# AdaLN-style adapter layer and LoRA feed-forward layer on one core: where the column registers are loaded, where the second chunk's weights are rounded, and where the bin sort runs

## The chip, the cores and the metric

One core of a Trainium2 chip runs the whole kernel. The metric is the device time of one execution in microseconds (us). The engines are named as in the profile: PE (matrix products) and PEld (its weight loads), DVE, ACT, POOL and SP. Each engine has its own instruction queue (DVEq, ACTq and so on), which also runs the register instructions. All engines work in parallel and meet only at semaphores.

## The reference

The input x has 64 items of 32 tokens with 512 features. Each item picks one of 8 weight matrices for the first layer (`a0`, values 3 to 7) and one of 16 adapters for the second (`a1`, values 2 to 6). Cut to what matters:

```python
# first layer
h0 = einsum('bsi,boi->bso', x, L0_cond_weight[a0])               # one 512x512 matrix per item
x  = x + h0 @ kernel + bias + lora(h0; 8 groups of 8 items) + shared_lora(h0)
# second layer: gated feed-forward, 512 -> 1376 -> 512, each product with the item's rank-16 adapter
gate = x @ W_gate.T + 0.5 * B_gate[a1] @ (A_gate[a1] @ x)
up   = x @ W_up.T   + 0.5 * B_up[a1]   @ (A_up[a1] @ x)
act  = silu(gate) * up
h    = act @ W_down.T + 0.5 * B_down[a1] @ (A_down[a1] @ act)
# routed linear layer: softmax over 4 ranks, top 1 selects a LoRA of that rank
out  = x + h @ W.T + b + routed_lora(h)
```

Which items share an adapter is data, so the kernel sorts the items on the chip and reaches an item's tokens through a column number that it holds in a register.

## The kernel before, in words

**Numbers.** Every fp32 operand is split in two fp32r parts, hi (rounded, written by ACT with `high`) and lo (the rest, x minus hi, written by DVE or POOL with `low`). A product is three matmuls (`product`, L1303 to L1305: hi*hi, lo*hi, hi*lo); a product with a small left side that holds hi and lo one above the other is two (`stacked`, L1309 and L1310).

**Stage 1, conditioning.** DVE sorts the 64 items by weight matrix into 22 blocks of 4 items (some slots are empty). For each block b, ACT and DVE load four column numbers (`item_cols`, L417) and split the block's tokens (`high_xs`, `low_xs`), PE multiplies (`cond`, L1373 to L1375: 12 matmuls), ACT (even b) or DVE (odd b) copies the result out, and POOL scatters it to a DRAM scratch. Between these, DVE runs a second sort, the bin sort, which puts the items in the order of the second layer's adapters: `fill_bins` ahead of block 0 (L1004), `find_fillers`, `rank_items`, `place_fillers`, `place_items` at blocks 13 to 16, then two small matmuls on PE after block 20 (L1384 to L1387), `item_places` and `gather_rows`. Each step of a sort waits for the one before it (`then`). The second block's tokens are split after block 0's weights, and `scatter_rows` lies between block 0's tokens and its weights.

**Stage 2, first layer.** Four passes t of 512 tokens (`first_layer`): PE transposes h0, multiplies it with the dense kernel and adds the LoRA part; DVE adds bias and residual (`add(0)` to `add(3)`). PE transposes the adapter rows of the second layer (`turn_a`) only after the four passes.

**Stage 3, second layer.** Four token blocks t of 512 tokens, each with 11 chunks fc of 128 hidden features (`chunks` calls `step`; chunk n = 11t + fc). A block opens with its tokens gathered in sorted order and split (`high_x1` on ACT, `low_x1` on DVE, 16 column slices each), `high_at`/`low_at`, then `ranks` and the masks (`open_tg`). Each chunk: PE transposes adapter rows (`turn_down`, L1515), gate product, up product, adapter parts, and the down product of the chunk before; ACT rounds the chunk's weights (`high_gu`, `high_bu`), `ad`, `dn`, computes silu and rounds act; DVE computes `low_bu`, lo of ad, act_f and act_lo; POOL computes gu_lo and dn_lo and issues the gathers of adapter rows two chunks ahead (`rows`). After the last chunk PE finishes block t (`td`, `bd`), ACT and DVE spread h back to the tokens' places (`put_h`, 16 column copies each), and only then do they begin the chunks of block t+1. In `high_x1`, `low_x1` and `put_h` the 16 column numbers are loaded four at a time (`bin_cols`, L423) between the slices. PE may not write the down product of block t+1 before `put_h(t)` is through (L1545, L1546).

**Stage 4, routed linear layer** (`routed`, `second_layer`), four passes of 512 tokens, which starts when `put_h(3)` is done.

The order on each engine is the order in which the code is written; nothing is planned at run time. The queues wait at semaphores in that order.

Of the kernel before, what the change touches and what calls it, by code (L numbers as in the profile page):

```python
# [21 lines left out]
F32 = mybir.dt.float32  # L22
# [103 lines left out]
def two_layers(nc, a, out):  # L126
    with ExitStack() as ctx:
# [127 lines left out]
        below = sb("below", [P, 2, N_ADP], F32)  # L255
        least = sb("least", [P, NBIN], F32)
        short = sb("short", [P, NBIN], F32)
        short_h = sb("short_h", [P, NBIN], F32)
        room = sb("room", [P, NBIN], F32)
        step_z = sb("step_z", [P, NBIN], F32)  # L260
# [4 lines left out]
        first4 = sb("first4", [P, NBIN], F32)  # L265
        end4 = sb("end4", [P, NBIN], F32)
# [363 lines left out]
        def _(act):  # L630
# [18 lines left out]
            def high_xs(b):  # L649
                at = item_cols(act, b)  # L650
# [20 lines left out]
            high_xs(1)  # L671
# [38 lines left out]
            high_h0(0)  # L710
# [12 lines left out]

# [15 lines left out]
            def high_x1(t):  # L739
# [12 lines left out]
            def put_h(t):  # L752
                act.wait_ge(S["h_ps"], C * t + 2)
                for q in range(TB // BT):
                    at = bin_cols(act, t * (TB // BT) + q)
                    for j in range(BI):
                        i = (q * BI + j) * ITEM_T
                        act.activation(h_all[:, 0:2, bass.ds(at[j], ITEM_T)], psD[:, 0:2, i:i + ITEM_T], ACT.Copy
                                       ).then_inc(S["h_out0"], 1)
# [9 lines left out]
            def body(t):  # L769
                def step(fc, j, par):  # L770
# [9 lines left out]
                    high(dn_hi[:, par, :], dn_raw[:], S["dn_hi_s"])  # L780
# [899 lines left out]
```

## Time and profile before

| | us |
|---|---|
| median of 3 runs (lowest, highest) | 784.01 (783.42, 784.02) |
| the profiled execution's own time | 782.84 |
| its span, first to last instruction | 780.9 |
| PE busy in the span | 704.9 (90%) |
| PEld, DVE, ACT, POOL busy | 586.1, 368.3, 289.4, 322.4 |

A row of a timeline or group has the start or the busy time in us, the engine, the line of the kernel, the operation, what it writes and reads, how many instructions (x4), and in brackets how long the engine had been idle before it and what ended that. "issue" means that the profile shows no other engine that it waited for. A line can be that of a helper (L838 is DVE's `low`, L632 ACT's `high`, L547 POOL's `low`), so tiles tell more. PEclk is PE's granted clock as a share of full speed; its two levels are 1.2 and 2.4 GHz (0.5 and 1.0).

### The profile page before, as it was taken

What the parts mean: (1) busy time and instruction counts of PE and PEld (TensorE: products, weight loads), DVE (VectorE), ACT (ScalarE), POOL (GpSimd) and SP (SyncE); (2) the same over time, 40 slices, a digit from 0 to 9 for tenths busy, and PEclk for the clock granted to TensorE, in tenths of its full rate; (3) what the DMA queues carried; (4) which work ended last, traced back from release to release, by engine and by line L of the source; (5) the groups of instructions that cost most, each with busy time, mean ns of one, the idle gap of its engine ahead of it and who ended that gap; (6) DMA issues with size and microseconds to landing.
All of it is one profiled execution on the core that took longest, in us unless ns stands there. A gap on an engine that the chain in (4) does not pass through costs nothing.

```text
span 780.9 us, 11491 instructions
## 1 busy us (share of the span) xinstructions
PE 704.9 (90%) x3432; PEld 586.1 (75%) x3432; DVE 368.3 (47%) x714; ACT 289.4 (37%) x605; POOL 322.4 (41%) x266
## 2 busy tenths in 40 slices
PE   4799899996999996799999779999977999977997
PEld 3577788875788885688888667888766888865775
DVE  5787755436424424533442554344254344324655
ACT  2775442115433324434332353333334433213220
POOL 0134350002876652385666167666318666400000
PEclk9999999997999998899999889999988999997999
DMA  8865271001443352143334124433314333200112
GB/s 321 320 226 187 98 282 55 1 0 42 136 151 122 121 195 72 49 134 122 121 121 131 45 71 140 130 117 99 125 41 122 121 122 121 74 0 2 55 55 107
DMA packets 30800, 88.90 MB, mean 114 GB/s; under 512 B 4608, under 2 KB 4736, under 8 KB 29216
## 3 DMA queue, kind: packets, MB, share of 16 engines
q1 hardware_dynamic: 21936, 61.05, 22.9%
q0 software_dynamic: 8672, 27.27, 10.8%
q8 instruction: 22, 0.36, 0.2%
q14 instruction: 26, 0.21, 0.1%
q10 hardware_dynamic: 144, 0.00, 0.0%
HBM read 78.35 MB, written 9.96 MB: 113 GB/s over the span
## 4 chain that ended last, share of the span: by engine, by line
PE 75%; DVE 9%; issue 5%; DVEq 4%; ACT 2%; ACTq 2%; DMA 1%; POOL 0%; SPq 0%; POOLq 0%
PE psD L1303 8%; PE psD L1304 8%; PE psD L1305 8%; PE psG L1303 5%; PE psG L1304 5%; PE psG L1305 5%; PE psU L1303 5%; PE psU L1304 5%; PE psU L1305 5%; DVEq L423 2%; PE psX L1303 2%; PE psX L1304 2%; PE psX L1305 2%; DVE tm L1142 2%; PE psD L1373 2%
## 5 line engine op out<-in xcount | busy, mean ns | idle before, releaser
L547 POOL TENSOR_TENSOR gu_lo<-gu_raw,gu_hi 128x1024 fp32r<-128x1024 f32 x44 | 105.7, 2402 | 211.2 <-ACT gu_hi L632 210.9
L838 DVE TENSOR_TENSOR bu<-ab,bu 64x512 fp32r<-64x512 f32 x44 | 84.2, 1913 | 66.3 <-ACT bu L632 66.0
L582 POOL DMA_INDIRECT ab<-in_ab,idx_row x88 | 87.0, 989 | 47.8 <-POOL idx_row L576 34.3
L1199 DVE TENSOR_TENSOR act_f<-psU,silu 128x512 f32<-128x512 f32 x44 | 30.3, 689 | 142.7 <-ACT silu L783 142.7
L783 ACT ACTIVATE silu<-psG 128x512 f32<-128x512 f32 x44 | 26.4, 599 | 158.8 <-PE psG L1310 158.7
L547 POOL TENSOR_TENSOR dn_lo<-dn_raw,dn_hi 128x512 fp32r<-128x512 f32 x44 | 69.2, 1572 | 26.2 <-ACT dn_hi L632 26.2
L1303 PE MATMUL psG<-x_hi,gu_hi 128*128 128x512 f32 x176 | 76.1, 432 | 0.0
L1304 PE MATMUL psG<-x_lo,gu_hi 128*128 128x512 f32 x176 | 71.9, 408 | 0.0
L1305 PE MATMUL psG<-x_hi,gu_lo 128*128 128x512 f32 x176 | 71.7, 407 | 0.0
L1303 PE MATMUL psD<-act_hi,dn_hi 128*128 128x512 f32 x176 | 69.0, 392 | 0.0
L1303 PE MATMUL psU<-x_hi,gu_hi 128*128 128x512 f32 x176 | 69.0, 392 | 0.0
L1304 PE MATMUL psD<-act_lo,dn_hi 128*128 128x512 f32 x176 | 69.0, 392 | 0.0
L1305 PE MATMUL psD<-act_hi,dn_lo 128*128 128x512 f32 x176 | 68.7, 390 | 0.0
L1304 PE MATMUL psU<-x_lo,gu_hi 128*128 128x512 f32 x176 | 68.6, 389 | 0.0
L1305 PE MATMUL psU<-x_hi,gu_lo 128*128 128x512 f32 x176 | 68.5, 389 | 0.0
L552 POOL DMA_INDIRECT h_scratch<-h,idx_s x22 | 25.5, 1161 | 68.7 <-DVE h L1033 34.9
L632 ACT ACTIVATE gu_hi<-gu_raw 128x1024 fp32r<-128x1024 f32 x44 | 46.2, 1050 | 3.3 <-DMA gu_raw<-in_gu 3.3
L632 ACT ACTIVATE act_hi<-act_f 128x512 fp32r<-128x512 f32 x44 | 27.8, 632 | 47.7 <-DVE act_f L1199 47.7
L1373 PE MATMUL psD<-cond_w_hi,xs_t_hi 128*128 x88 | 36.6, 416 | 9.5 <-DVE cond_w_lo L838 7.4
L838 DVE TENSOR_TENSOR act_lo<-act_f,act_hi 128x512 fp32r<-128x512 f32 x44 | 30.6, 695 | 30.7 <-ACT act_hi L632 30.7
L1305 PEld LDWEIGHTS psG<-x_hi,gu_lo 128*128 128x128 f32 x176 | 35.0, 199 | 8.4
L1304 PEld LDWEIGHTS psG<-x_lo,gu_hi 128*128 128x128 f32 x176 | 35.2, 200 | 6.1
(321 smaller groups left out, 1622.9 us busy)
## 6 DMA issues: line engine op xcount, KB each, us to landing
gu_raw<-in_gu SPq DMA_DIRECT2D x44, 512.0 KB, 3.5
dn_raw<-in_dn SPq DMA_DIRECT2D x44, 256.0 KB, 3.1
cond_w_raw<-in_cond_w SPq DMA_DIRECT2D x8, 1024.0 KB, 5.7
x_all<-in_x_t SPq DMA_DIRECT2D x4, 1024.0 KB, 9.9
tok<-h_scratch SPq DMA_DIRECT2D x4, 1024.0 KB, 7.2
out_t<-x_all SPq DMA_DIRECT2D x16, 256.0 KB, 2.2
ab<-in_ab,idx_row POOLq DMA_INDIRECT x88, 3.2
kraw<-in_kern SPq DMA_DIRECT2D x1, 1024.0 KB, 12.3
```

Of the source, the lines that this page charges most:

```text
L423: _, at = nc.values_load_multi_w_load_instructions(item1_at[0:1, b * BI:b * BI + BI], engines=[eng.engine], min_val=0, max_val=TOKENS - IT ...
L547: pool.tensor_tensor(dst, x, hi, ALU.subtract).then_inc(s, 1)
L552: pool.indirect_dma_start(h0_dram, bass.IndirectOffsetOnAxis(idx_s[:, b:b + 1], 0), h0[:, ring, :], None).then_inc(S[f"c_st{ring}"], 16)
L582: pool.indirect_dma_start(ab[:, par, g, :], None, a["ab"], bass.IndirectOffsetOnAxis(idx_row[:, par, g:g + 1], 0)).then_inc(S[f"ab_in{par} ...
L632: act.activation(dst, x, ACT.Copy).then_inc(s, 1)
L783: act.activation(silu[:], psG[:], ACT.Silu).then_inc(S["silu_s"], 1)
L838: dve.tensor_tensor(dst, x, hi, ALU.subtract).then_inc(s, 1)
L1199: dve.tensor_tensor(act_f[:], psU[:], silu[:], ALU.mult).then_inc(S["act_f_s"], 1)
L1303: pe.matmul(ps, wh, xh, start=start, stop=False, skip_group_check=True)
L1304: pe.matmul(ps, wh, xl, start=False, stop=False, skip_group_check=True)
L1305: return pe.matmul(ps, wl, xh, start=False, stop=stop, skip_group_check=True)
L1373: pe.matmul(ps, xh, w[0], start=c == 0, stop=False)
```

## The change

The bin sort leaves stage 1 except for its two counts, which are copied to tiles of their own (`keep_counts`). `count_bins` runs after stage 1, the other parts in the gaps of the four passes of stage 2, and the two small matmuls go to PE between `kern(0)` and `kern(1)` of the last pass. In front of block 0 both engines load the columns of two blocks first, then split both blocks' tokens, then the weights; `scatter_rows` goes ahead of the tokens. The last pass of stage 2 takes in `turn_a(0)` on PE, and `block_cols`, `low_at(0)` and `low_bu(0, 0)` on DVE. `block_cols` loads all 16 columns of a token block at once: for `high_x1`/`low_x1(t+1)` in chunk 9 of block t, for `put_h(t)` in chunk 10, ahead of the wait for silu's input. ACT rounds gu of chunk 0 of block t+1 after td_hi, and gu and bu of its chunk 1 before `put_h(t)` and no longer in chunk 0. The kernel adder of stage 1 moves from block 11 to 12.

```diff
+        rank1 = sb("rank1", [ITEMS, N_ADP], F32)
+        count1 = sb("count1", [P, N_ADP], F32)
...
-        def bin_cols(eng, b):
-
-            _, at = nc.values_load_multi_w_load_instructions(item1_at[0:1, b * BI:b * BI + BI], engines=[eng.engine],
-                                                             min_val=0, max_val=TOKENS - ITEM_T)
-            return at
+        def block_cols(eng, t):
+
+            cols = []
+            for b in range(TB // BT * t, TB // BT * (t + 1)):
+                _, at = nc.values_load_multi_w_load_instructions(item1_at[0:1, b * BI:b * BI + BI], engines=[eng.engine],
+                                                                 min_val=0, max_val=TOKENS - ITEM_T)
+                cols += at
+            return cols
...
             act.wait_ge(S["item_ready"], 1)
-            act.wait_ge(S["x_all_in"], 16 * NTB)
-            high_xs(0)
+            cols = item_cols(act, 0), item_cols(act, 1)
             folded(2)
             folded(3)
+            act.wait_ge(S["x_all_in"], 16 * NTB)
+            high_xs(0, cols[0])
+            high_xs(1, cols[1])
             act.wait_ge(S["w_in0"], 16)
...
-                for q in range(TB // BT):
-                    at = bin_cols(act, t * (TB // BT) + q)
-                    for j in range(BI):
-                        i = (q * BI + j) * ITEM_T
-                        high(x1_hi[:, :, i:i + ITEM_T], x_all[:, :, bass.ds(at[j], ITEM_T)], S["x1_hi_s"])
+                for j, col in enumerate(at):
+                    i = j * ITEM_T
+                    high(x1_hi[:, :, i:i + ITEM_T], x_all[:, :, bass.ds(col, ITEM_T)], S["x1_hi_s"])
...
             act.wait_ge(S["item1_ready"], 1)
+            taken = block_cols(act, 0)
             high_at(0)
             high_gu(0, 0, 0)
             high_bu(0, 1)
-            high_x1(0)
+            high_x1(0, taken)
             high_tg(0, 0)
             high_tg(0, 1)
+            high_gu(1, 1, 0)
+            high_bu(1, 1)
...
-                    if not last(fc):
+                    if not first and not last(fc):
                         high_gu(1 - par, n + 1, n)
                         high_bu(1 - par, (NF // 2 + par) * t + j + par + 1)
...
+                    if last(fc, 1) and t < NTB - 1:
+                        taken.extend(block_cols(act, t + 1))
+                    if last(fc):
+                        placed.extend(block_cols(act, t))
                     act.wait_ge(S["gate_ps"], n + 1)
...
                 if t < NTB - 1:
-                    high_x1(t + 1)
+                    high_x1(t + 1, taken)
                     high_at(t + 1)
-                    high_gu(0, NF * t + NF, NF * t + NF)
                 act.wait_ge(S["td_m"], t + 1)
                 high(td_hi[:], tm[:, 1, :], S["td_hi_s"])
                 if t < NTB - 1:
+                    high_gu(0, NF * t + NF, NF * t + NF)
                     high_bu(0, (NF // 2 + 1) * (t + 1) + 1)
                     high_tg(t + 1, 0)
                     high_tg(t + 1, 1)
-                put_h(t)
+                    high_gu(1, NF * t + NF + 1, NF * t + NF)
+                    high_bu(1, NF // 2 * (t + 1) + 1)
+                put_h(t, placed)
...
             dve.wait_ge(S["item_ready"], 1)
-            low_xs(0)
+            cols = item_cols(dve, 0), item_cols(dve, 1)
             scatter_rows()
+            keep_counts()
+            low_xs(0, cols[0])
+            low_xs(1, cols[1])
...
-                if b == 11:
+                if b == 12:
...
-                if b == 13:
-                    find_fillers()
-                if b == 14:
-                    rank_items()
-                if b == 15:
-                    dve.wait_ge(S["small_in"], 32)
-                    place_fillers()
-                if b == 16:
-                    place_items()
...
+                if t == 0:
+                    fill_bins()
+                if t == 1:
+                    gather_rows()
+                    rank_items()
+                if t == 2:
+                    place_items()
+                if t == 3:
+                    item_places()
                 add(0)
                 add(1)
                 if t < NTB - 1:
                     low_h0(t + 1)
+                else:
+                    taken.extend(block_cols(dve, 0))
+                    low_at(0)
+                    low_bu(0, 0)
                 add(2)
+                if t == 0:
+                    find_fillers()
+                if t == 1:
+                    dve.wait_ge(S["small_in"], 32)
+                    place_fillers()
                 add(3)
...
-            pe.wait_ge(S["item1_ready"], 1)
-            pe.wait_ge(S["mask1_ready"], 1)
...
                 kern(0)
+                if t == NTB - 1:
+                    pe.wait_ge(S["t0_m"], NTB)
+                    pe.wait_ge(S["perm1_s"], 1)
+                    pe.matmul(psX[:, 0:ITEMS], cst("item_no", ITEMS), perm1[:], start=True, stop=True)
+                    pe.matmul(psX[:, ITEMS:2 * ITEMS], cst("ones", ITEMS), perm1_f[:], start=True, stop=True
+                              ).then_inc(S["pos1_ps"], 1)
                 kern(1)
...
                 if t < NTB - 1:
                     turn_h0(t + 1)
+                else:
+                    turn_a(0)
```

DVE's `body` changes as ACT's does (`block_cols(dve, ...)` stands between the lo part of ad and the wait for silu), and `low_x1` and `put_h` take the list of columns in the same way.

## Rows read from the trace of the kernel before

**Rows 1.** Page, part 2: PE's granted clock in 40 slices of 19.5 us, tenths.

```profile
PEclk9999999997999998899999889999988999997999
```

**Rows 2.** PE's waits, whole span: us in total, times, longest.

```profile
PE psX L1515 <- DVE ad L838: 17.9, 6, 4.9
PE psX L1303 <- DVE at_lo L838: 17.8, 3, 7.5
PE psX L1303 <- DVE hta_lo L838: 10.0, 1, 10.0
...
PE psD L1373 <- DVE cond_w_lo L838: 7.4, 1, 7.4
```

**Rows 3.** Windows: us, then busy of PE, PEld, DVE, ACT, POOL, PEclk, DMA, GB/s.

```profile
286.50:340.10 53.60, 41.20 (x207) 35.56 (x206) 25.35 (x54) 20.41 (x56) 21.72 (x18) 0.87 0.28 89
419.20:471.90 52.70, 41.09 (x208) 35.10 (x206) 28.42 (x56) 22.32 (x58) 23.38 (x18) 0.87 0.23 71
551.00:602.70 51.70, 41.74 (x208) 35.96 (x207) 24.02 (x54) 20.68 (x57) 21.76 (x19) 0.87 0.23 71
```

**Rows 4.** Windows: a stretch inside a block, narrow matmuls, a slow-clock stretch.

```profile
220.00:290.00 70.00, 70.00 (x355) 59.26 (x355) 25.48 (x29) 25.29 (x43) 44.18 (x38) 1.00 0.44 147
...
313.00:316.00 3.00, 3.00 (x27) 3.00 (x26) 2.60 (x4) 0.63 (x1) 0.00 (x0) 1.00 0.00 0
...
327.70:333.00 5.30, 5.29 (x14) 4.24 (x15) 1.15 (x2) 2.63 (x3) 4.21 (x5) 0.50 0.69 213
```

**Rows 5.** DVE timeline, chunks 9 and 10 of block 0: act_f.

```profile
283.59 0.69 DVE L1199 TENSOR_TENSOR act_f<-psU,silu 128x512 f32<-128x512 f32 x1 [4.22 <-ACT silu L783]
...
293.47 0.69 DVE L1199 TENSOR_TENSOR act_f<-psU,silu 128x512 f32<-128x512 f32 x1 [5.87 <-ACT silu L783]
```

**Rows 6.** Line 423, whole span: the queue's load of four columns, ns.

```profile
L423 DVEq TENSOR_LOAD <-item_at x32: 339/343/355, 175.8 to 703.9; - x32
```

**Rows 7.** DVE timeline at the first block change.

```profile
302.98 3.04 DVE L838 TENSOR_TENSOR x_lo<-x_all,x_hi 128x128 fp32r<-128x128 f32 x4 [1.14 <-issue]
...
317.57 0.69 DVE L838 TENSOR_TENSOR bu<-ab,bu 64x512 fp32r<-64x512 f32 x1
...
320.50 0.62 DVE L1170 COPY h_all<-psD 128x64 f32 x4 [1.40 <-issue]
```

**Rows 8.** ACT timeline, same stretch.

```profile
321.11 0.57 ACT L758 ACTIVATE h_all<-psD 128x64 f32 x4 [1.07 <-issue]
```

**Rows 9.** DVE timeline: low_bu of chunk 2 beside POOL; wf_lo in block 2.

```profile
334.85 3.38 DVE L838 TENSOR_TENSOR bu<-ab,bu 64x512 fp32r<-64x512 f32 x1 [5.30 <-ACT bu L632]
...
462.41 7.41 DVE L838 TENSOR_TENSOR wf_lo<-wf_raw,wf_hi 128x2048 fp32r<-128x2048 f32 x1 [2.90 <-ACT rb L632]
```

**Rows 10.** PE timeline, where block 0's ranks begin.

```profile
181.19 0.55 PE L1303 MATMUL psX<-x_hi,at_hi 128*128 128x256 f32 x1 [6.15 <-DVE x_lo L838]
```

**Rows 11.** The first weight load, SP's queue: issue, and time to landing.

```profile
L464 SPq DMA_DIRECT2D cond_w_raw<-in_cond_w x1: 383/383/383, 12.5 to 12.5; - x1
...
DMA to landing us min/median/max: 7.5/7.5/7.5
```

**Rows 12.** Timeline of the opening: ACT's first tokens, DVE's first weights.

```profile
19.06 0.91 ACT L632 ACTIVATE xs_t_hi<-x_all 128x128 fp32r x4 [6.97 <-issue]
...
23.39 2.49 DVE L838 TENSOR_TENSOR cond_w_lo<-cond_w_raw,cond_w_hi 128x512 fp32r<-128x512 f32 x4
```

**Rows 13.** PE timeline: first matmul of conditioning blocks 1, 14 and 21.

```profile
29.49 0.39 PE L1373 MATMUL psD<-cond_w_hi,xs_t_hi 128*128 x1
...
65.82 0.46 PE L1373 MATMUL psD<-cond_w_hi,xs_t_hi 128*128 x1
...
89.21 0.50 PE L1373 MATMUL psD<-cond_w_hi,xs_t_hi 128*128 x1
```

**Rows 14.** DVE timeline, pass 0: the gap before add(0).

```profile
115.78 1.41 DVE L1101 SCALAR_TENSOR_TENSOR x_all<-psD,bias,x_all 128x512 f32<-128x512 f32 x2 [3.09 <-PE psD L1310]
```

**Rows 15.** Window of the second half of fill_bins (eleven small DVE instructions).

```profile
16.20:18.60 2.40, 0.73 (x2) 0.01 (x1) 2.16 (x11) 0.00 (x0) 0.00 (x0) 1.00 1.04 428
```

More of the change, by code:

```diff
@@ L708, in high_h0, with high_gu, high_bu, high_at @@
                     high(HT0[t % 2][0][:, c, :], H0_BANK[c][:], S["h0t_hi"])
+            def high_gu(par, n, free):
+                act.wait_ge(S["gu_in"], 16 * (n + 1))
+                act.wait_ge(S["up_ps"], free)
+                high(gu_hi[:, par, :], gu_raw[:], S["gu_hi_s"])
+            def high_bu(par, gathers):
+                act.wait_ge(S[f"ab_in{par}"], 16 * NGT * gathers)
+                high(bu[:, par], ab[:, par, :, P:STAB], S["bu_hi_s"])
+            def high_at(t):
+                for g in range(NGT):
+                    act.wait_ge(S["at_ps"], NGT * t + g + 1)
+                    high(at_hi[:, g, :], A_BANK[g][:], S["at_hi_s"])
             high_h0(0)
@@ L750, in high_tg, with put_h @@
                 high(tg_hi[:, k, :], tm[:, k, :], S["tg_hi_s"])
-            def put_h(t):
+            def put_h(t, at):
                 act.wait_ge(S["h_ps"], C * t + 2)
[L754 to L759, printed above, removed]
+                for j, col in enumerate(at):
+                    i = j * ITEM_T
+                    act.activation(h_all[:, 0:2, bass.ds(col, ITEM_T)], psD[:, 0:2, i:i + ITEM_T], ACT.Copy
+                                   ).then_inc(S["h_out0"], 1)
             act.wait_ge(S["item1_ready"], 1)
+            taken = block_cols(act, 0)
             high_at(0)
@@ L909, in _, with keep_counts, count_bins @@
             across = [P, NBIN, N_ADP]
-            def fill_bins():
+            def keep_counts():
+                dve.wait_ge(S["count1_ps"], 1)
+                both(dve.tensor_copy(rank1[:], psU[0:ITEMS, 0:N_ADP]),
+                     dve.tensor_copy(count1[:], psU[:, N_ADP:2 * N_ADP]))
+            def count_bins():
                 then(dve.tensor_tensor(tri[:], cst("adapter_no").unsqueeze(1).broadcast_to(across),
                                        cst("adapter_no").unsqueeze(2).broadcast_to(across), ALU.is_le))
-                dve.wait_ge(S["count1_ps"], 1)
-                count = psU[:, N_ADP:2 * N_ADP]
-                then(dve.tensor_scalar(miss[:, 1], count, float(-BI), 0.0, ALU.add, ALU.max))
-                then(dve.scalar_tensor_tensor(out=miss[:, 0], in0=miss[:, 1], scalar=float(BI), in1=count,
+                then(dve.tensor_scalar(miss[:, 1], count1[:], float(-BI), 0.0, ALU.add, ALU.max))
+                then(dve.scalar_tensor_tensor(out=miss[:, 0], in0=miss[:, 1], scalar=float(BI), in1=count1[:],
                                               op0=ALU.add, op1=ALU.subtract))
@@ L951, in rank_items @@
             def rank_items():
-                then(dve.tensor_tensor(qm[:], psU[0:ITEMS, 0:N_ADP], room[0:ITEMS], ALU.add))
+                then(dve.tensor_tensor(qm[:], rank1[:], room[0:ITEMS], ALU.add))
                 then(dve.tensor_tensor(qo[:], qm[:], onehot1[:], ALU.mult))
@@ L1128, in low_at, with low_bu, low_x1 @@
                     low(at_lo[:, g, :], A_BANK[g][:], at_hi[:, g, :], S["at_lo_s"])
-            def low_x1(t):
-                for q in range(TB // BT):
-                    at = bin_cols(dve, t * (TB // BT) + q)
-                    for j in range(BI):
-                        i = (q * BI + j) * ITEM_T
-                        dve.wait_ge(S["x1_hi_s"], TB // ITEM_T * t + q * BI + j + 1)
-                        low(x1_lo[:, :, i:i + ITEM_T], x_all[:, :, bass.ds(at[j], ITEM_T)],
-                            x1_hi[:, :, i:i + ITEM_T], S["x1_lo_s"])
+            def low_bu(par, n):
+                dve.wait_ge(S["bu_hi_s"], n + 1)
+                low(bu[HALF:P, par], ab[HALF:P, par, :, P:STAB], bu[HALF:P, par], S["bu_lo_s"])
+            taken = []
+            for t in range(NTB):
+                first_layer(t)
+            def low_x1(t, at):
+                for j, col in enumerate(at):
+                    i = j * ITEM_T
+                    dve.wait_ge(S["x1_hi_s"], TB // ITEM_T * t + j + 1)
+                    low(x1_lo[:, :, i:i + ITEM_T], x_all[:, :, bass.ds(col, ITEM_T)], x1_hi[:, :, i:i + ITEM_T],
+                        S["x1_lo_s"])
             def masked(dst, ps, r, t, s):
@@ L1162, in open_tg, with put_h @@
                 low_tg(t, 1)
[L1164 removed]
+            def put_h(t, at):
                 dve.wait_ge(S["h_ps"], C * t + C)
[L1166 to L1173 removed]
+                for j, col in enumerate(at):
+                    i = j * ITEM_T
+                    dve.tensor_copy(h_all[:, 2:4, bass.ds(col, ITEM_T)], psD[:, 2:4, i:i + ITEM_T]
+                                    ).then_inc(S["h_out1"], 1)
             dve.wait_ge(S["x1_f"], C * NTB)
[L1175 to L1176 removed]
+            low_x1(0, taken)
             dve.wait_ge(S["mask1_ready"], 1)
             open_tg(0)
[L1180 to L1184 removed]
             def body(t):
+                taken, placed = [], []
                 def step(fc, j, par):
@@ L1195, in step @@
                         S["ad_lo_s"])
+                    if last(fc, 1) and t < NTB - 1:
+                        taken.extend(block_cols(dve, t + 1))
+                    if last(fc):
+                        placed.extend(block_cols(dve, t))
                     dve.wait_ge(S["silu_s"], n + 1)
@@ L1222, in body @@
                     low_bu(0, NF * t + NF)
-                put_h(t)
+                put_h(t, placed)
             for t in range(NTB):
@@ L1456, in first_layer @@
                 lora(3)
-            for t in range(NTB):
-                first_layer(t)
             def turn_a(t):
@@ L1470, in turn_a @@
                     mm.then_inc(S["at_ps"], 1)
+            for t in range(NTB):
+                first_layer(t)
             def ranks(t):
-                pe.wait_ge(S["t0_m"], NTB)
+                pe.wait_ge(S["item1_ready"], 1)
+                pe.wait_ge(S["mask1_ready"], 1)
                 pe.wait_ge(S["ad_lo_s"], NF * t)
@@ L1483, in ranks @@
                 mm.then_inc(S["tg_ps"], 1)
-            turn_a(0)
             ranks(0)
```

60 lines of the change are left out of this document (14 added, 46 removed).

## The prediction

> **What bounds the kernel now.** I read the page first. PE is busy 90% of the span, and the row of its granted clock has dips that come back at even distances [rows 1]. Then PE's waits: the reader is to see four causes, which do not lie in the chunks but between stages: ad_lo (17.9 us in 6 waits), at_lo (17.8 in 3), hta_lo (10.0, once), the first weights (7.4, once) [rows 2]. Inside a block PE never waits: 70 us of 70 at full clock [rows 4], and a chunk takes 293.47 - 283.59 = 9.88 us [rows 5]. So the time to win lies at the three block changes, at the two ends of the second layer, and in conditioning.
>
> The windows from the last chunk's `turn_down` to that of chunk 2 of the next block show what one change costs: 53.6, 52.7 and 51.7 us with the clock at 0.87 on average [rows 3]. Their work on PE at full clock is three chunks (29.6), 48 matmuls of 256 columns for `ranks` and `bd` (27 matmuls take 3.0 us [rows 4], so 5.8 with their weights) and 8 transposes (0.9): 36.3 us. The other 15 to 17 us are a wait for x1_lo and at_lo (5 to 7.5), a wait for ad_lo behind `put_h` (4.6 to 4.9), and PE at 1.2 GHz when it comes back [rows 2, 4]: in 327.7 to 333.0 it is at 0.5 and does 14 matmuls in 5.3 us.
>
> What makes both waits long is not the slices themselves. The four copies of a `put_h` group take 0.62 us, then DVE idles 1.40 and ACT 1.07 with no releaser [rows 7, 8]: that is the queue loading four columns, of which the load proper is 0.343 [rows 6]. A group costs 2.0 us on DVE and 1.6 on ACT, so 16 slices take 8.1 and 6.5.
>
> **The block changes.** (1) `block_cols` costs 4 x about 1.5 = 6.0 us of DVE's queue and 4 x about 1.24 = 5.0 of ACT's (the idle above plus some 0.1 to set up the first slice). It lies in chunks 9 and 10 between ad and silu's wait. There DVE idles 4.2 us in chunk 9, after a low_bu during which the queue is already free (2.5 us), and 5.87 in chunk 10 [rows 5]; DVE's next instruction is due 6.1 us after the queue is free, so the loads fit with 0.1 to 0.2 us to spare. If they overrun, act_f(10) comes late by the overrun, and with it the chain below. Cost taken: 0. (2) The slices then follow each other every 0.2 us: 16 in 3.2 us. Worked from the end of act_lo(10) at 295.5: x1_lo done at 298.8, td mask 299.4, at_lo 300.6. PE ends the last down product at 300.6, so `ranks` starts at about 300.8 and not at 308.1. Since high_gu(0) now stands behind td_hi, POOL's gu_lo no longer falls on the last x_lo slices, which took 3.04 us for four [rows 7]. (3) ranks and bd run at full clock to 306.6; tg_lo is done 4.3 us after ranks (as before), at 308.2; gu_hi(1), bu_hi(1) at 309; `put_h` runs 309 to 311 on both engines; low_bu(1) and ad_lo(0) end at 312.2, and PE asks for ad_lo(0) at 313.1. The second wait is gone, and with it the second slow stretch. (4) Chunk 2: its low_bu waits for the gather (about 319.3) and meets POOL's gu_lo and dn_lo back to back, as in the 3.38 us of [rows 9]; ad_lo(1) at about 323.4 against PE's 323.1: 0.3 us.
>
> So a change takes 36.3 + about 0.7 for starts and the first wait + 0.3 = 37.3 us, against 53.6 and 51.7: -16.3 and -14.4. At the second change DVE also computes wf_lo, 7.4 us because POOL holds it off [rows 9]. With chunk 1 at full clock PE comes for chunk 2 two us sooner, and DVE has wf_lo, ra_lo, rb_lo and low_bu ahead of ad_lo(1). Best case no wait (-15.4), worst 3.6 us (-11.8); I take -13.4. Sum of the three: -44.1.
>
> Here the Trainium skill bears on the trace (SBUF — State Buffer, Who interferes with whom): a DVE instruction with two SBUF inputs and a GpSimd one that reads SBUF exclude each other for the whole instruction, and whoever starts first wins. It speaks against this change, which brings gu_lo(1) forward onto low_bu(0) and low_bu(1). This trace agrees, 0.69 us becoming 3.38.
>
> The same skill (DMA: Bandwidth & Descriptors, Latency and other measured facts) gives a `tensor_load` floor of about 600 ns; the row has 343. By the page `block_cols` would overrun its cover by some 1 us and the sum would be 3 us smaller; the row decides.
>
> **The start.** Before: x_all is there, ACT loads columns, splits block 0 at 19.06, folds, rounds weights from 20.8; DVE has fill_bins (2.2 us of it in [rows 15]), its columns, block 0's lo, then scatter_rows, so w_lo starts at 23.39 and PE at 24.32 [rows 12]. The first weights land at 12.5 + 7.5 = 20.0 [rows 11]. After: columns are loaded by 16.6, scatter_rows and keep_counts done by 18.9, both blocks' lo by 20.6, w_hi of the first quarter 20.05 to 20.7, w_lo from 20.75. PE starts at 21.7: -2.6.
>
> **Conditioning's tail.** Blocks 1 to 14 take (65.82 - 29.49)/13 = 2.79 us each, blocks 14 to 21 (89.21 - 65.82)/7 = 3.34 [rows 13], since the chained sort steps keep DVE's queue from loading columns ahead. Without them PE sets the pace: 7 x 0.55 = 3.8, and 0.6 for the two matmuls taken out; the wait for g_lo returns about 0.2 less: -4.4 in all (the 0.6 is within 3.54 of the last block). kfold's adder at block 12 is covered by two blocks of slack.
>
> **The four passes.** DVE idles 3.09 us before add(0) [rows 14], about 2.4 before add(3). fill_bins takes 2.4, find_fillers 2.1, gather_rows with rank_items 2.1, place_fillers 1.1, place_items 1.2: each fits its gap. Cost 0; without the cover up to 1 us per pass. POOL's gathers for block 0 start some 30 us later but are due 25 us after that. The two matmuls and `turn_a(0)` go through PE here: they move, they add nothing.
>
> **Block 0's opening.** PE waits 6.15 us and 1.1 [rows 10]. The slices shrink from 8.1 to 3.2, but add(2) and add(3) now stand behind 6.0 us of column loads, low_at and low_bu, so the last add is some 1.4 us later than PE would allow, and PE already did turn_a. On before's clock PE starts ranks at 180.1 (181.19 before) and ends them 2.2 earlier; chunk 0 keeps that: -2.3 (bounds -1.5 and -4, by how long PE stays at 1.2 GHz).
>
> **The end.** put_h(3) on DVE: 16 copies at 0.14 = 2.2 us after h at 697.9 in place of 8.2: -6.0. PE's idle shrinks from 10.0 [rows 2] to 4, so it still comes back at half clock, a little shorter: -6.2.
>
> **Sum.** -44.1 - 2.6 - 4.4 - 2.3 - 6.2 = -59.6. Against the profiled execution's 782.84: 723.2. The median of the runs lies 1.2 above that execution, so 724.4.
>
> **Rivals.**
> A. The port between DVE and POOL takes the second wait's place. POOL's gu_lo(1) and dn_lo(0) (2.4 + 1.3 us) run where low_bu(0), low_bu(1) stand, and a low_bu lost 2.7 us of this kind [rows 9]. Two such losses in a row delay ad_lo(0) by 3 to 5 us, PE falls back to 1.2 GHz for one stretch (some 2 us): 6.5 us per change, +20: 744. For: the rows. Against: my times leave 0.9 us of slack and one loss at most.
> B. The columns are not loaded under cover: the queue waits for the engine, or the loads run late. Seven preloads of 6.0 us (three in chunk 9, four in 10) come onto DVE's chain: +42: 766. Against: low_bu's 0.69 in [rows 7] ran while the queue was loading (the first group of put_h starts 0.2 us behind it).
> C. Slower: 32 columns don't stay in registers and are fetched again at each use. It decides as soon as a use costs a load plus address (0.34 + about 0.3 us) in place of a share of a group (0.5 on DVE): 16 uses then take 10.6 and not 8.1, twice per change, with the preload on top (6.0, twice): +17 per change in place of -15, +5 at each end: 782.8 + 51 + 10 - 7 = 837, say 838. Against: nothing in the trace shows a limit.
> D. It changes nothing: the waits have other causes than the column loads. 784. Against: the idle with no releaser.
>
> **How the numbers follow.** Forecast 0.62 (own range 718 to 732), A 0.22 (732 to 750), B 0.10, C 0.03, D 0.02; 0.01 for less than 718. 724.4 is the forecast's. The range 717 to 744 holds the forecast and most of A. No change means within 0.2% (1.6 us), about what a measurement can tell: 0.01; slower 0.04 (C and half of D); faster 0.95.
>
> **What would show it.** In the trace of after: first conditioning matmul near 21.7; blocks 14 to 21 at 2.8 us; the wait of `ranks` under 0.5 us at the three changes; no wait of L1515 near 4.9; windows of a change near 37 us with the clock at 1.0; about 4 us before the routed layer. Wrong if DVE's act_f(10) starts much later than 6 us after ad_lo, if low_bu(1) takes over 3 us, or if the clock still dips at the changes.

## The result, and the profile after

The changed kernel takes 725.19 us (median of 4 runs, 724.72 to 725.93) against 783.95 for the kernel before (783.42 to 784.02): a ratio of 0.9253, 95% interval 0.9237 to 0.9269. Its profiled execution took 725.00, with a span of 723.1 (before: 780.9), so the two spans differ by 57.8 us. PE is now busy 95% of the span.

The page's row of PE's granted clock answers to [rows 1]. The dips at even distances are gone; what is left is the slice in which block 0 opens and the one in which the routed layer begins.

```profile
PEclk9999999998999999999999999999999999998999
```

PE's waits in the changed kernel, whole span (us in total, times, longest), answer to [rows 2]. The first row of the view, 8.4 us for the start of the first sort (8.0 before), is left out:

```profile
...
PE psD L1402 <- DVE cond_w_lo L853: 5.6, 1, 5.6
PE psX L1332 <- DVE x_lo L853: 5.0, 1, 5.0
PE psX L1545 <- DVE ad L853: 4.4, 3, 2.7
PE psX L1332 <- DVE hta_lo L853: 4.0, 1, 4.0
...
PE psX L1332 <- DVE at_lo L853: 0.7, 3, 0.3
```

The waits for ad_lo (releaser `ad`) were 17.9 us and are 4.4; those for at_lo were 17.8 and are 0.7. The same three windows as in [rows 3], from the last chunk's `turn_down` to chunk 2's, and then the wait and the first 12 matmuls of the routed layer (columns as in rows 3):

```profile
277.83:314.93 37.10, 36.80 (x208) 31.53 (x206) 20.55 (x53) 18.79 (x55) 20.93 (x17) 1.00 0.38 116
394.03:434.01 39.98, 36.95 (x208) 31.54 (x206) 24.37 (x56) 21.32 (x58) 22.69 (x18) 1.00 0.28 86
513.14:550.25 37.11, 36.80 (x207) 31.68 (x206) 20.39 (x54) 19.53 (x56) 20.56 (x17) 1.00 0.29 88
...
649.45:654.61 5.16, 5.16 (x13) 2.89 (x13) 1.66 (x3) 2.68 (x6) 0.00 (x0) 0.50 0.02 5
```

In the first and third change PE's busy time and the window's length are now nearly one number (36.80 of 37.10), the clock is 1.00 in all three, and the second change is 2.9 us longer than its neighbours.

DVE's timeline at the first change (start, us, engine, line, operation; in brackets the idle time before and what ended it):

```profile
284.82 0.69 DVE L1228 TENSOR_TENSOR act_f<-psU,silu 128x512 f32<-128x512 f32 x1 [5.87 <-ACT silu L796]
...
286.82 3.31 DVE L853 TENSOR_TENSOR x_lo<-x_all,x_hi 128x128 fp32r<-128x128 f32 x16
...
299.67 0.69 DVE L853 TENSOR_TENSOR bu<-ab,bu 64x512 fp32r<-64x512 f32 x1
300.39 2.19 DVE L1201 COPY h_all<-psD 128x64 f32 x16
302.62 0.69 DVE L853 TENSOR_TENSOR bu<-ab,bu 64x512 fp32r<-64x512 f32 x1
```

In [rows 7] `put_h` showed as groups of four, all but the first behind some 1.40 us in which nothing released DVE. Now 16 copies are one run of 2.19 us, and 16 slices of x_lo one run of 3.31. act_f of the last chunk still comes straight behind silu, with the same 5.87 of idle time as in [rows 5]: the column loads disappeared into it. The queue's own rows show them there, in chunk 9 (first row) and chunk 10 (second row); behind the durations stand the starts of the first and of the last of the four groups:

```profile
L429 DVEq TENSOR_LOAD <-item_at x4: 340/342/346, 268.8 to 273.3; - x4
...
L429 DVEq TENSOR_LOAD <-item_at x4: 339/340/341, 278.7 to 283.1; - x4
```

### The profile page after: what moved, and what is told of

It is laid out like the page before. It is cut to its first block, busy times and chain, and to the rows that moved or that the text cites. A ratio compares the mean times of both kernels' runs of the same rounds, so it can differ in the third digit from the quotient of the medians.

```text
span 723.1 us, 11495 instructions
## 1 busy us (share of the span) xinstructions
PE 689.0 (95%) x3432; PEld 574.2 (79%) x3432; DVE 350.6 (48%) x716; ACT 286.0 (40%) x605; POOL 317.4 (44%) x266
## 3 DMA queue, kind: packets, MB, share of 16 engines
HBM read 78.35 MB, written 9.96 MB: 122 GB/s over the span
## 4 chain that ended last, share of the span: by engine, by line
PE 84%; DVE 4%; DMA 3%; issue 3%; ACT 2%; DVEq 1%; POOL 1%; ACTq 0%; SPq 0%; POOLq 0%
PE psD L1332 10%; PE psD L1333 10%; PE psD L1334 9%; PE psG L1332 6%; PE psG L1334 5%; PE psG L1333 5%; PE psU L1333 5%; PE psU L1334 5%; PE psU L1332 5%; PE psX L1332 2%; PE psX L1333 2%; PE psX L1334 2%; PE psD L1402 2%; PE psD L1403 1%; PE psD L1404 1%
## 5 line engine op out<-in xcount | busy, mean ns | idle before, releaser
L554 POOL TENSOR_TENSOR gu_lo<-gu_raw,gu_hi 128x1024 fp32r<-128x1024 f32 x44 | 107.8, 2451 | 130.9 <-ACT gu_hi L639 130.7
L853 DVE TENSOR_TENSOR bu<-ab,bu 64x512 fp32r<-64x512 f32 x44 | 74.8, 1699 | 74.5 <-ACT bu L639 74.3
L554 POOL TENSOR_TENSOR dn_lo<-dn_raw,dn_hi 128x512 fp32r<-128x512 f32 x44 | 67.4, 1533 | 30.6 <-ACT dn_hi L639 29.9
L1332 PE MATMUL psG<-x_hi,gu_hi 128*128 128x512 f32 x176 | 72.8, 414 | 0.2
L1333 PE MATMUL psG<-x_lo,gu_hi 128*128 128x512 f32 x176 | 68.9, 392 | 0.0
L1334 PE MATMUL psG<-x_hi,gu_lo 128*128 128x512 f32 x176 | 68.9, 392 | 0.0
L1334 PE MATMUL psD<-act_hi,dn_lo 128*128 128x512 f32 x176 | 68.6, 390 | 0.0
L559 POOL DMA_INDIRECT h_scratch<-h,idx_s x22 | 23.8, 1082 | 63.7 <-ACT h L668 32.4
L639 ACT ACTIVATE bu<-ab 128x512 fp32r<-128x512 f32 x44 | 27.4, 622 | 36.7 <-DMA ab<-in_ab,idx_row 36.7
L1334 PEld LDWEIGHTS psG<-x_hi,gu_lo 128*128 128x128 f32 x176 | 33.2, 189 | 7.7
```

Source lines behind the costliest of these rows:

```text
L554: pool.tensor_tensor(dst, x, hi, ALU.subtract).then_inc(s, 1)
L559: pool.indirect_dma_start(h0_dram, bass.IndirectOffsetOnAxis(idx_s[:, b:b + 1], 0), h0[:, ring, :], None).then_inc(S[f"c_st{ring}"], 16)
L639: act.activation(dst, x, ACT.Copy).then_inc(s, 1)
L853: dve.tensor_tensor(dst, x, hi, ALU.subtract).then_inc(s, 1)
L1332: pe.matmul(ps, wh, xh, start=start, stop=False, skip_group_check=True)
L1333: pe.matmul(ps, wh, xl, start=False, stop=False, skip_group_check=True)
```

## The experiments

Each kernel is the changed kernel with one edit, unless said otherwise. Times are medians, with the ratio to the kernel before timed on the same chip. Where two medians are about 1 us apart, windows of the traces are compared too.

**late_columns: the registers loaded where they are used.**

```diff
-                for j, col in enumerate(at):
+                for j in range(TB // ITEM_T):
+                    col = four_cols(act, t, at, j)
...
-                        taken.extend(block_cols(act, t + 1))
-                        placed.extend(block_cols(act, t))
```

four_cols loads four columns at every fourth slice; the edit is the same in `high_x1`, `low_x1` and both `put_h`.

> The changed kernel, but the column registers of x1 and put_h are loaded where they are used, four at a time, as before; order of the weights, sort and start as changed. My theory (the column loads are most of what the block changes cost): at each change the last x_lo comes 4.9 us later (8.1 for 3.2), so ranks waits about 5; put_h on DVE takes 8.2 and not 2.2, so ad_lo(0) comes some 5 later; PE comes back at half clock twice, about 2 us in all. 12 to 13 per change, 38 in three; at the end +6; at the opening the slices cost 4.9 more but the last two additions no longer stand behind 6.0 us of loads, about +1. 725.2 + 45 = 770. Rival (the new order of the weights gave at least half of the 44 us): the changes get no more than 22 us longer, 754 or less.

Measured: 766.09 us, ratio 0.9787 [0.9761, 0.9812]. PE's waits and the three windows of this kernel:

```profile
PE psX L1335 <- DVE at_lo L859: 15.6, 3, 5.3
PE psX L1548 <- DVE ad L859: 13.7, 6, 3.9
PE psX L1335 <- DVE hta_lo L859: 10.0, 1, 10.0
```

```profile
280.62:330.72 50.10, 40.95 (x208) 35.22 (x206) 22.99 (x54) 21.18 (x57) 23.25 (x19) 0.90 0.33 103
409.76:459.66 49.90, 40.12 (x208) 34.48 (x206) 24.78 (x56) 22.08 (x58) 22.02 (x18) 0.90 0.22 70
538.76:588.05 49.29, 40.41 (x208) 34.93 (x206) 22.54 (x54) 20.62 (x57) 22.18 (x19) 0.90 0.25 74
```

Both waits are back, the clock falls again (0.90), and the three changes take 149.3 us against 114.2: 35.1 of the 43.8 us that they gained, where I expected 38. The second wait is 3.6 to 3.9 us where the kernel before has 4.6 to 4.9, and ACT's order is what still differs there. The rival (at most 22) falls.

**old_order: ACT rounds chunk 1's weights in chunk 0 again, behind `put_h`.**

```diff
-                    if not first and not last(fc):
+                    if not last(fc):
                         high_gu(1 - par, n + 1, n)
...
-                    high_gu(1, NF * t + NF + 1, NF * t + NF)
-                    high_bu(1, NF // 2 * (t + 1) + 1)
                 put_h(t, placed)
```

`high_gu` of chunk 0 also goes back ahead of td_hi.

> The changed kernel, but ACT rounds gu and bu of chunk 1 in chunk 0 behind put_h, and gu of chunk 0 ahead of td, as before; the columns are loaded early. My theory (the order is worth little by itself once put_h takes 2.2 us): gu_hi(1) and bu_hi(1) come about 2 us later than in the changed kernel, POOL's gu_lo(1) then lies on low_bu(1), ad_lo(0) is late by 0 to 2 us: +0 to 2 per change, +1 to +5 in all, 728. Rival (the order is what removes the second wait): ad_lo waits about 5 us at each change and the clock falls, +6 to 7 each, 745.

Measured: 728.37 us, ratio 0.9312 [0.9284, 0.9340]. DVE and POOL at the first change, from the timeline:

```profile
301.75 2.13 DVE L849 TENSOR_TENSOR bu<-ab,bu 64x512 fp32r<-64x512 f32 x1
...
300.92 2.41 POOL L554 TENSOR_TENSOR gu_lo<-gu_raw,gu_hi 128x1024 fp32r<-128x1024 f32 x1 [8.03 <-ACT gu_hi L639]
```

low_bu(1) ends only after POOL's gu_lo(1), as forecast. The windows took 37.32, 41.71 and 38.65 us, 3.5 more in all, and the chunk after the second one 11.53 at a clock of 0.85 where the changed kernel has 9.96. So at the changes the order by itself gives 8.7 us with late columns (43.8 - 35.1), and 3.5 with early ones. The slow chunk makes it 5, but it is not shown to belong to the order: in one_group_more, whose order is that of the changed kernel, the same chunk is slow too.

**one_group_more: a fifth group of four columns in the last chunk.**

```diff
                     if last(fc):
+                        item_cols(dve, 0)
                         placed.extend(block_cols(dve, t))
```

The same on ACT.

> The changed kernel with a fifth group of four columns loaded in the last chunk of each block, on DVE and ACT; its values are not used. My theory (the four groups fill DVE's idle stretch to within 0.1 us): act_f of the last chunk comes 1.4 us later, and x_lo, at_lo and ranks with it: +1.4 at each of three changes, nothing at the end (the last down product has 1.6 us of slack), 729.5; if PE's wait of about 1.6 us lets the clock fall at the changes, 733 to 735. Rival (the queue has room to spare): 725.2, within 0.7.

Measured: 729.74 us, ratio 0.9320 [0.9292, 0.9348]. DVE's ad and act_f of the last chunk, and PE's `ranks` (timeline):

```profile
278.46 0.29 DVE L854 TENSOR_TENSOR ad<-psX,ad 128x128 fp32r<-128x128 f32 x1 [0.55 <-ACT ad L639]
...
285.98 0.69 DVE L1230 TENSOR_TENSOR act_f<-psU,silu 128x512 f32<-128x512 f32 x1 [7.23 <-issue]
...
293.36 0.36 PE L1334 MATMUL psX<-x_hi,at_hi 128*128 128x256 f32 x1 [1.58 <-DVE at_lo L854]
```

The idle time grows from 5.87 to 7.23 and its releaser changes from silu to "issue", the queue itself. A group costs about 1.49 us on DVE (in the changed kernel four groups start 1.47 to 1.50 us apart), 1.36 of it comes through, so four groups left 0.13 us of cover. `ranks` waits 1.6 us instead of 0.2 at each change. Ahead of the routed layer, where I expected no loss, this trace is 1.1 us longer too (21.26 us from the last chunk's `turn_down`, against 20.16). The clock did not fall at the changes (0.99 to 1.00).

**sort_back: the bin sort in conditioning.**

```diff
+                if b == 9:
+                    count_bins()
+                if b == 10:
+                    fill_bins()
...
+                if b == 13:
+                    find_fillers()
+                if b == 14:
+                    rank_items()
```

> The changed kernel with the bin sort back in conditioning: count_bins and fill_bins at blocks 9 and 10, the other steps at blocks 13 to 16, places and gather_rows behind block 21, PE's two small matmuls ahead of block 21. My theory (chained sort steps keep DVE's queue from loading columns ahead, and the four passes hid them): blocks 14 to 21 take 3.3 us again in place of 2.72, +4.4, and up to 1 for the two steps at 9 and 10: 730. Rival (the four passes pay for the sort in the changed kernel): the passes get 1 to 4 us shorter here, so 726 to 729 or less.

Measured: 735.27 us, ratio 0.9394 [0.9366, 0.9423]: a miss by 5 us. PE's timeline, first matmuls of blocks 12 to 15:

```profile
58.41 0.49 PE L1402 MATMUL psD<-cond_w_hi,xs_t_hi 128*128 x1
...
63.62 0.49 PE L1402 MATMUL psD<-cond_w_hi,xs_t_hi 128*128 x1 [2.21 <-DVE xs_t_lo L853]
...
70.95 0.50 PE L1402 MATMUL psD<-cond_w_hi,xs_t_hi 128*128 x1 [3.14 <-DVE xs_t_lo L853]
...
75.39 0.39 PE L1402 MATMUL psD<-cond_w_hi,xs_t_hi 128*128 x1
```

Three blocks take 5.2, 7.3 and 4.4 us in place of 2.8: my reading is that two more chained steps, put there by me, used up DVE's lead, so that the steps at 13 to 16 hit PE at once. Up to the aeff product conditioning took 12.4 us more than in the changed kernel (75.7 against 63.4), which says nothing of the kernel before, where those two steps stood at the start. The next two kernels mend that.

**start_back and start_and_sort_back: the start of before, without and with the sort where it was.**

```diff
             dve.wait_ge(S["item_ready"], 1)
-            cols = item_cols(dve, 0), item_cols(dve, 1)
+            low_xs(0)
             scatter_rows()
-            keep_counts()
-            low_xs(0, cols[0])
-            low_xs(1, cols[1])
...
+            low_xs(1)
```

`keep_counts`, `count_bins` and `fill_bins` stand ahead of this, `low_xs(1)` behind the first weights, and ACT goes likewise.

> The changed kernel with the start of before: on ACT block 0's tokens, folds, weights, then block 1's tokens, columns loaded where used; on DVE count_bins and fill_bins first, block 0's lo ahead of scatter_rows, the first weights, then block 1's lo. The other sort steps stay in the four passes. My theory (order of the start: DVE reaches the first weights late): first conditioning matmul at about 24.3 as in the kernel before, against 21.9 to 22.8 in the five traces with the new start, so +1.5 to +2.4, less some 0.3 for the two sort steps that leave conditioning's end and pass 0: 727. Rival (the start is set by when x and the weights land, which differs from run to run): first matmul within 0.5 of 22.4, 725.2.

> start_back with the whole sort where it was before: find_fillers, rank_items, place_fillers, place_items at blocks 13 to 16, places and gather_rows behind block 21, PE's two small matmuls ahead of block 21. Beside start_back this is the sort's place alone. My theory: blocks 14 to 21 take 3.3 us each again in place of 2.72 (+4.4 with the matmuls), the four passes get 0.8 shorter (as in the trace of sort_back): start_back + 3.6, about 731. Rival (from sort_back, which was 10 us slower than the changed kernel: chained steps in conditioning cost far more than that): start_back + 8 or more, 735.

Measured: 728.73 us, ratio 0.9309 [0.9289, 0.9330], and 732.35, 0.9347 [0.9323, 0.9371]. PE's first matmul of conditioning in each:

```profile
25.13 0.79 PE L1400 MATMUL psD<-cond_w_hi,xs_t_hi 128*128 x1 [8.06 <-DVE cond_w_lo L852]
```

```profile
25.46 0.79 PE L1399 MATMUL psD<-cond_w_hi,xs_t_hi 128*128 x1 [8.07 <-DVE cond_w_lo L852]
```

With the new start that first matmul stood at 21.67 to 23.80 in ten traces (median 22.4) and the wait was 4.7 to 6.6 us; so by these two traces the start is worth 2.7 to 3.0 us, and with the same start it moves by 2 from one execution to another. The kernel before, with nearly the start of these two, began at 24.32, which would give 1.9. For the sort, conditioning from its first matmul to the aeff product takes 64.2 us without it and 68.6 with it: +4.4. The four passes take 74.1 and 73.25: they paid 0.8 for it, about 0.6 of that for the two small matmuls by the prediction's price. Net 3.6, the difference of the medians 3.6, as expected.

**second_spread: ra and rb rounded in block 3, wf left in block 2's first chunk.** (The three are weights of the routed layer.)

```diff
                     if first and t == 2:
...
                         low(wf_lo[:], wf_raw[:], wf_hi[:], S["wf_lo_s"])
-                        low(ra_lo[:], ra_raw[:], ra_hi[:], S["wf_lo_s"])
...
+                    if last(fc, 1) and t == NTB - 1:
+                        dve.wait_ge(S["wf_hi_s"], 3)
+                        low(ra_lo[:], ra_raw[:], ra_hi[:], S["wf_lo_s"])
```

rb goes with ra, and their high halves on ACT too.

> The changed kernel with the second layer's roundings spread: wf stays in chunk 0 of block 2, ra and rb move to block 3's last chunk but one, where block 3 loads no columns, on ACT and DVE. My theory (the one wait of 2.7 us of PE inside a change is for ad_lo of chunk 2 behind wf_lo, ra_lo and rb): DVE has 4.3 us less in front of it, the wait goes to 0.3, and the new place hides ra and rb in 4 to 5 us of idle time: -2.4, 722.8. Rival (POOL's gu_lo and dn_lo back to back hold DVE off whatever the order): wf_lo alone ends as late, less than 1 us gained.

Measured: 723.80 us, ratio 0.9261 [0.9241, 0.9280]. The wait went from 2.69 to 2.17 us, not to 0.3. DVE and POOL, timeline:

```profile
423.92 6.95 DVE L854 TENSOR_TENSOR wf_lo<-wf_raw,wf_hi 128x2048 fp32r<-128x2048 f32 x1 [2.06 <-ACT wf_hi L639]
...
422.70 2.42 POOL L554 TENSOR_TENSOR bd_lo<-fix_b,bd_hi 128x1024 fp32r<-128x1024 f32 x1
425.06 2.40 POOL L554 TENSOR_TENSOR gu_lo<-gu_raw,gu_hi 128x1024 fp32r<-128x1024 f32 x1
427.42 1.28 POOL L554 TENSOR_TENSOR dn_lo<-dn_raw,dn_hi 128x512 fp32r<-128x512 f32 x1
```

My theory fell and the rival stood: wf_lo began while bd_lo ran and ended at 430.87, about 2.2 us after POOL's last of three. Taking 1.1 us of work (ra_lo 0.43, rb 0.69) off DVE changed little, since what counts is who holds the port that DVE and POOL share.

**second_late: all three rounded in block 3's last chunk but one, where POOL is quiet.** 

```diff
-                    if first and t == 2:
...
                     if last(fc, 1) and t == NTB - 1:
                         dve.wait_ge(S["wf_hi_s"], 3)
+                        low(wf_lo[:], wf_raw[:], wf_hi[:], S["wf_lo_s"])
                         low(ra_lo[:], ra_raw[:], ra_hi[:], S["wf_lo_s"])
```

> The changed kernel with wf, ra and rb all rounded in block 3's last chunk but one, on ACT and DVE, none in chunk 0 of block 2. My theory (in second_spread wf_lo started at 423.92 and ended at 430.9, just when POOL's bd_lo, gu_lo and dn_lo, back to back from 422.70, were through: what made chunk 2 wait was where wf_lo stood, not how much DVE had to do): in block 3 POOL ends dn_lo at about 623 and has nothing but index work until 630, so wf_lo takes 2.2 to 2.5 us, DVE's three roundings 3.3 us in a gap of 4.2, and PE's wait at the second change is 0.3 us or less: the changed kernel - 2.5. Rival (the wait has another cause or turns up in block 3): the same time as the changed kernel, within 0.7.

Measured beside **after_again**, the changed kernel on the same chip:

> The changed kernel itself, timed beside the two below so that differences of 1 us can be told: 725.2, within 0.7, or whatever this chip gives; the others are compared with it.

720.32 us, ratio 0.9206 [0.9186, 0.9225], against 724.47, 0.9265 [0.9245, 0.9285]. DVE's timeline in second_late:

```profile
621.07 2.29 DVE L853 TENSOR_TENSOR wf_lo<-wf_raw,wf_hi 128x2048 fp32r<-128x2048 f32 x1 [1.22 <-ACT rb L639]
623.28 0.43 DVE L853 TENSOR_TENSOR ra_lo<-ra_raw,ra_hi 128x272 fp32r<-128x272 f32 x1
623.75 0.69 DVE L853 TENSOR_TENSOR rb<-rb_raw,rb 64x512 fp32r<-64x512 f32 x1
```

wf_lo takes 2.29 us, and the second change 37.12 like the others: -2.9. The medians differ by 4.2. In the two profiled executions the stretch from the second change on has another 0.9 us in it, nearly all in the first 12 matmuls of the routed layer: 5.16 us in after_again, and in second_late

```profile
647.11:651.30 4.19, 4.19 (x13) 2.43 (x13) 1.66 (x3) 2.67 (x6) 0.00 (x0) 0.64 0.01 2
```

behind the same wait of 4.03 us. In other executions the wait at the second change can cost more than its length: nine traces of this study have a wait of 2.2 to 4.2 us there, and in four of them the chunk behind it took 11.3 to 11.6 us, in the other five 9.9 to 10.0. In the two traces without the wait it took 10.0. The clock of these chunks, of one that fell (one_group_more) and one that didn't (after_again):

```profile
436.59:447.90 11.31, 11.31 (x50) 9.49 (x51) 3.60 (x6) 5.18 (x8) 8.02 (x8) 0.87 0.53 157
```

```profile
432.31:442.24 9.93, 9.93 (x50) 8.42 (x51) 3.59 (x6) 5.30 (x8) 7.41 (x7) 1.00 0.53 157
```

In after_again's own trace that chunk was not slow, so whether slow chunks make up the rest of the 1.3 us in its other executions is not shown.

**three_edits and best: the columns of block 0 and h of the second layer earlier.** three_edits stands on second_spread, best on second_late.

```diff
+                if t == NTB - 1:
+                    taken.extend(block_cols(dve, 0))
                 add(0)
                 add(1)
...
+                    if t == 0 and c == 2:
+                        act.wait_ge(S["h_out1"], ITEMS)
                     high(HT2[t % 2][0][:, c, :], h_all[:, c, tokens_of(t)], S["h_hi_s"])
```

DVE waits for PE ahead of add(0) anyway. `low_bu(0, 0)` goes behind add(2), and ACT's wait for DVE's `put_h` no longer stands ahead of `high_h(0)`.

> second_spread with two more edits: in the last pass DVE loads block 0's columns ahead of add(0), while it waits for PE anyway, and rounds bu behind add(2); before the second layer ACT rounds h of the first two feature groups as soon as its own put_h is done, and waits for DVE's put_h only ahead of the third. My theory: the last addition comes 1.85 us earlier and ranks with it (PE waits 3.2 and not 5.0), PE's wait ahead of the routed layer goes from 4.0 to 3.1: second_spread - 2.7, 720.1. Rival (the adds are not what ranks waits for, or the clock gives it back): within 0.7 of second_spread.

> second_late with the two other edits of three_edits (block 0's columns ahead of add(0); h of the first two groups rounded ahead of DVE's put_h). Theory: the gains add, since they lie in different waits of PE: -2.5 - 1.75 - 0.75 = 5.0 below the changed kernel, 720.2 if that takes 725.2. Rival (the clock or the start gives part back): 3.5 or less below it.

Measured: three_edits 720.29 us, ratio 0.9203 [0.9188, 0.9219]; best 716.96, ratio 0.9162 [0.9144, 0.9180]. PE's waits in best, and its windows of the second change and of the first 12 routed matmuls:

```profile
...
PE psD L1405 <- DVE cond_w_lo L854: 4.9, 1, 4.9
PE psX L1335 <- DVE hta_lo L854: 3.3, 1, 3.3
PE psX L1335 <- DVE x_lo L854: 3.3, 1, 3.3
PE psX L1548 <- DVE ad L854: 1.7, 2, 0.9
```

```profile
391.10:428.23 37.13, 36.80 (x207) 31.53 (x206) 20.81 (x53) 18.79 (x55) 20.93 (x17) 1.00 0.27 84
...
642.98:645.78 2.80, 2.80 (x13) 1.73 (x13) 1.66 (x3) 2.34 (x5) 0.00 (x0) 1.00 0.03 9
```

`ranks` of block 0 waits 3.3 us in both kernels and the routed layer 3.3, as expected. three_edits is 3.5 us faster than second_spread, against 2.7 expected, and best 7.5 faster than the changed kernel on the same chip, against 5.0. The windows of best give 2.9 + 1.7 + 0.75, and in the profiled execution 2.36 more because the routed matmuls ran at full clock (2.80 us; 5.16 in the changed kernel, and 5.15 at 0.50 in three_edits behind the same wait of 3.28). What decides which of the two happens behind such a wait stays open.

## Why the prediction was right, step by step

Each stage is measured between the same two matmuls of PE in both traces; the chunks inside the blocks and the rest of the routed layer take the same time within 0.2 us.

| step | forecast | measured |
|---|---|---|
| block changes | -16.3, -13.4, -14.4 | -16.5, -12.7, -14.6 |
| start, to the first conditioning matmul | -2.6 | -1.5 |
| conditioning, to the aeff product | -4.4 | -5.2 |
| first layer to chunk 2 of block 0 | -2.3 | -2.0 |
| last chunk to the routed layer's first product with wf | -6.2 | -5.5 |
| sum | -59.6 | -57.8 in the span, -58.8 in the medians |

**The column loads.** The price of a group read from rows 7 and 8, and the step that 16 loads fit under DVE's idle stretch with 0.1 to 0.2 us left, both hold: late_columns gives 35.1 us back, one_group_more finds 0.13. In chunk 9 the loads ran over a little, as rival B had it: act_f started 0.26 us late at the first and third change, on time at the second, and in second_late 1.15 late at the first; PE's chunk took 9.88 us all the same. Rival B's other half, that the queue waits for the engine, is out: low_bu of chunk 9 ran from 267.92 to 270.40 and the first load began at 268.8.

**The changes.** 37.10 us against 37.3 forecast. low_bu of chunk 2 met POOL's roundings as foreseen (3.53 us at the first change), and no wait of PE's matmuls shows behind it, only 0.27 us of PEld's; forecast 0.3. Rival A was wrong in its place: gu_lo(1) started at 299.94, behind low_bu(0), ran beside `put_h` and took 2.68 us for its 2.40; neither low_bu lost a turn. It was right as a mechanism: old_order, in which gu_lo(1) comes 1.9 us later, loses 1.4 us on low_bu(1).

**The second change.** Forecast at -13.4, came at -12.7, inside its bounds. My reason was the length of DVE's list. second_spread shows that this was the wrong reason for the right size. In the changed kernel's own trace the port is seen from both sides:

```profile
426.28 2.52 DVE L853 TENSOR_TENSOR wf_lo<-wf_raw,wf_hi 128x2048 fp32r<-128x2048 f32 x1 [2.90 <-ACT rb L639]
428.73 2.63 DVE L853 TENSOR_TENSOR ra_lo<-ra_raw,ra_hi 128x272 fp32r<-128x272 f32 x1
...
427.27 3.78 POOL L554 TENSOR_TENSOR gu_lo<-gu_raw,gu_hi 128x1024 fp32r<-128x1024 f32 x1 [0.63 <-ACT gu_hi L639]
```

Here POOL had a gap of 0.63 us, wf_lo took it and ran in 2.52, and gu_lo lost 1.4; then ra_lo, 0.43 us by itself, took 2.63. The Trainium skill (SBUF — State Buffer, Who interferes with whom) says that the first to start wins; these rows agree, and [rows 9], second_spread and second_late (7.41, 6.95 and 2.29 us for one instruction) add that against several POOL instructions back to back the loser waits for the last.

**The start.** The term furthest off for its size. I had the first weights rounded from 20.05, by one landing time [rows 11]; in this execution ACT waited for them until 21.23, and PE began at 22.84:

```profile
21.23 2.19 ACT L639 ACTIVATE cond_w_hi<-cond_w_raw 128x512 fp32r<-128x512 f32 x4 [0.70 <-DMA cond_w_raw<-in_cond_w]
```

Against the median of ten traces the new order is worth 1.9 to 3.0: one profile of each kernel can't size a term that hangs on when a transfer lands.

**Conditioning.** -5.2 against -4.4. Blocks 14 to 21 take 2.72 us each, where I had 2.79, and with what follows block 21 they give 4.7; another 0.5 lies in block 0 (4.66 us for 5.17), which I had not counted, and which is not shown to be the change's: the ten traces with the new start have 4.2 to 5.25 there. The sort's place by itself is worth 4.4, by start_and_sort_back beside start_back. With the start the two are -6.7, forecast -7.0.

**The four passes and block 0's opening.** The size came right, -2.0 for -2.3; the working was off in two places. I took the 0.6 us of the two small matmuls out of conditioning and put nothing into the passes, since they only move; the sort costs the passes 0.8. So `ranks` of block 0 starts 0.3 us earlier behind the aeff product than before, and not 1.1. The rest came from `ranks` to chunk 0, 1.9 us shorter: its second wait of 1.1 is gone, and what the other 0.8 is was not measured. three_edits shows that the column loads ahead of the last additions still cost 1.7.

**The end.** PE's wait fell from 10.0 to 4.0 as forecast. The step "it still comes back at half clock, a little shorter" was wrong in its last three words: the same 12 matmuls took 4.71 us before and 5.16 after. They differ by execution, though: behind the same wait of 4.0 us they took 4.19 us in second_late and 4.36 in old_order.

C and D are out: 16 slices run in 3.3 us on columns loaded more than 5 us before, and late_columns moves the time by 41 us.

**Luck.** The second change's size is luck, since the reason behind it did not hold. The profiled execution was forecast at 723.2 and took 725.0; the misses of the terms (+1.1 at the start, -0.8 in conditioning, +0.7 each at the second change and at the end) partly cancel. The 1.2 us added for the way from the profiled execution to the median was 0.2 here, which brought the median's forecast, 724.4, within 0.8 of 725.2.

## What to carry to other kernels

A gap of an engine in which nothing released it may be its queue loading registers for addresses that were known long before; load them in a stretch where the engine waits for something else, and size that stretch to the tenth of a microsecond. When an elementwise instruction takes three times its usual time, look at what another engine runs beside it before shortening the list in front of it: moving it to a quiet chunk gained 2.9 us, removing its neighbours 0.5. A wait of PE can cost more than its length, when the clock falls behind it, so of two waits that are equally long the one that PE returns from at half clock is the one to remove; look at it in several executions, since the clock behind one and the same wait differed between them here.

## What the runs showed of the hardware

- A group of four register loads costs DVE's queue about 1.49 us and ACT's about 1.24 (in the changed kernel the groups start 1.47 to 1.50 and 1.23 us apart; 1.36 came through for the fifth group), of which the load proper is 0.34 on DVE [rows 6].
- The queue runs such loads while the engine works. In one_group_more act_f began 7.52 us after ad began (285.98 - 278.46), and five groups take about 7.45 (5 x 1.49): they start with ad, not behind its end. In chunk 9 of the changed kernel the first load began at 268.8, while low_bu was running (267.92 to 270.40) and before ad (270.43).
- PE's clock behind a wait is not settled by the wait's length alone: after 2.7 us it was 0.85 to 0.87 over the next chunk in three executions of nearly the same program and 1.00 in three others, and after 3.28 us the routed matmuls ran at 0.50 in one kernel and at 1.00 in another.
